# Weights quantised wholly beside the convolution, squares and layer norm sums on ScalarE, input turned by DMA

## The chip, the cores and the metric

One core of a Trainium2 chip runs the whole program in one launch. The metric is device time in microseconds, from the first instruction to the last. Engines are named as the profile names them: PE (matrix products), PEld (its weight loads), DVE (vector), ACT (scalar), POOL (GpSimd), SP (the engine that issues the DMAs here).

## The reference

```python
x = x + tanh(g_xattn[0]) * ssm(ctx, ctx, layernorm(x))          # x, ctx: [8, 512, 1024]
x = x + tanh(g_ffn[0]) * ffn(layernorm(x))
# ssm(k, v, q): 64 heads of 8 channels, sequence length 1024
kv  = einsum('bhil,bhjl->bijhl', k, v)                          # k = v = ctx here
out = causal_conv(kv, ssm_kernel[h]) + kv * D[h]
out = einsum('bijhl,bhil->bjhl', out, q)
# ffn: 1024 -> 4096 -> 1024; mx_quant: blocks of 32 along the contraction share a power of two
h = bf16(layernorm(x) * w + b)
h = gelu(bf16(mx_quant(h) @ mx_quant(W1) + b1))
h = bf16(mx_quant(h) @ mx_quant(W2) + b2)
ffn = bf16(x + h)
```

## The kernel before, in words

Two blocks run one after the other, with a barrier between them. Each engine has its own instruction list, in an order written out by hand; semaphores are the only link.

**The convolution block** (`mixer_block`) goes over 64 heads; two heads share a tile of x (32 tiles). For head h:
- ACT copies k into PSUM (`copy_k`). DVE multiplies it with shifted k into `kk`, 8 blocks of 4.5 diagonals of 64 columns (`make_kk`). ACT rounds `kk` to `kk_hi` (`high_half`), DVE makes the rest `kk_lo` (`low_half`). `kk` exists once, `kk_hi` and `kk_lo` twice.
- PE (`conv_stretch`) multiplies a Toeplitz slab of the taps, loaded by SP from `taps_scratch`, with `kk_hi` and `kk_lo` into a row of 2304 columns of PSUM (`y_ps`), in five stretches from the end of the row: 72 matmuls a head. After stretch 1 the upper part (blocks 5 to 7) is complete, at the end the lower part (blocks 0 to 4).
- DVE multiplies each part with q (`times_q`: part 0 is blocks 5 to 7, part 1 is blocks 0 to 4). POOL adds up the products in seven additions for each part (`sum_part`). PE turns the sums back, DVE adds x (`residual`, at odd heads), SP stores x1.
- At even heads DVE takes the layer norm statistics of the next x tile (`ln_stats`) and ACT applies them (`ln_apply`); at odd heads PE turns the result (`turn_q`) and ACT copies it out (`take_q`).

DVE's order in head h is: `times_q(h-1, 1)`, `make_kk(h+1)`, `ln_stats` (even) or `residual` (odd), `times_q(h, 0)`, `low_half(h+1)`, then a piece of weight work. That piece is, for heads 0 to 31, the block maxima of one weight tile (`weight_maxima`, 1 MB each), at head 32 also the scales of all weights (`weight_scales`), and from head 32 on the quantisation of one tile of W2 for each two heads: integers at the even head, clip and scale at the odd one (`layer2_ints`, `layer2_clip`, `layer2_quant`). In PSUM `y_ps` begins 256 columns into a bank.

**The FFN block** (`ffn_block`) goes over 16 groups of two x1 tiles (256 rows). For group g PE runs `layer1(g, b)` for 16 banks (256 matmuls) and then `layer2` of the two tiles of group g-1 (256 matmuls). ACT adds the bias and applies gelu; DVE takes statistics, weighs and quantises the input of group g+1 (`weigh_input`, `quantise_input`), takes the peaks of the hidden values (`peak`), quantises them (`hidden_ints`, `hidden_clip`, `hidden_quant`), and finishes the output tiles (`second_bias`, `gated_sum`). The quantised input `hq` is turned by PE (`turn_input`, 8 transposes for a tile, between the parts of `layer2`) and copied by ACT (`keep_input`) into `xq_T`, which exists once. In group 0 DVE also quantises the 16 tiles of W1, PE turns them (`turn_weights`) and ACT keeps them (`keep_w1`). SP loads x1 tiles (`load_tile`), stores an output tile (`store`, which waits for `gated_sum`) and loads the next tile into the same buffer (`reload`, which waits until that store has landed).

Of the kernel before, what the change touches and what calls it, by code (L numbers as in the profile page):

```python
# [16 lines left out]
P = 128  # L17
B = 8
# [17 lines left out]
W_BUFS = 4  # L36
# [3 lines left out]
L1_BANKS = 3  # L40
# [22 lines left out]
def mixer_block(nc, x_t, ctx_e, taps_in, skip_in, g_x, scratch, x1_t, w_m, w_raw, w_inv, w2_t, w2_raw, w2_int, w2_q,  # L63
                first_loads, tiles):

# [7 lines left out]
    half = tiles // 2  # L73
    stretches = [(max(end - 512, 0), end) for end in range(row, 0, -512)]
    with ExitStack() as stack:
# [6 lines left out]
        def sem(name):  # L82
# [3 lines left out]
        taps = sb("taps", [HEADS, PADK], F32)  # L86
        taps_hi = sb("taps_hi", [HEADS, PADK], F32R)
# [15 lines left out]
        stats = sb("stats", [P, 2, 6], F32)  # L103
        mean_var = sb("mean_var", [P, 2], F32)
# [30 lines left out]
        stats_ready, aggr_ready, var_ready, rstd_ready = sem("stats_ready"), sem("aggr_ready"), sem("var_ready"), sem("rstd_ready")  # L135
# [9 lines left out]
        def _(sp):  # L145
# [42 lines left out]
            sp.wait_ge(kk_ready, 1)  # L188
            load_k(2)
            for t in range(2, X_SLOTS):  # L190
                load_x(t)
            load_w(0)
            load_w(1)
            for h in range(heads):
# [11 lines left out]
                if 1 <= h < tiles - 1:  # L206
                    sp.wait_ge(w_max_ready, h)
                    load_w(h + 1)
                if h in (tiles - 2, tiles - 1):
                    load_w2(h - (tiles - 2))  # L210
                if t > half:
                    if h % TILE_HEADS == 0:
                        store_w2(t - half - 1)
                    elif t + 1 < tiles:
                        load_w2(t - half + 1)
# [11 lines left out]
        def _(pe):  # L227
            def conv_stretch(h, i):
# [7 lines left out]
                if i == 1 and h >= 1:  # L236
                    pe.wait_ge(products_ready, 2 * h)
# [43 lines left out]
        def _(act):  # L281
# [24 lines left out]

            def ln_apply(t):
# [3 lines left out]
                if t >= 1:  # L311
# [833 lines left out]
```

## Time and profile before

| | us |
|---|---|
| median of 3 runs (2044.01 to 2044.49) | 2044.43 |
| the profiled execution's own time | 2045.5 |
| its span | 2043.7 |
| PE busy | 1931.1 (94%) |
| DVE busy | 1735.5 (85%) |
| POOL busy | 967.6 (47%) |
| ACT busy | 735.7 (36%) |
| mean granted clock of PE | 0.977 |

Durations below come from the profiled execution. An engine's busy time says only how much it did; what sets the end is the wait that ends last in each stage. Idle time in square brackets stands before an instruction and names what ended it.

### The profile page before, as it was taken

What the parts mean: (1) busy time and instruction counts of PE and PEld (TensorE: products, weight loads), DVE (VectorE), ACT (ScalarE), POOL (GpSimd) and SP (SyncE); (2) the same over time, 40 slices, a digit from 0 to 9 for tenths busy, and PEclk for the clock granted to TensorE, in tenths of its full rate; (3) what the DMA queues carried; (4) which work ended last, traced back from release to release, by engine and by line L of the source; (5) the groups of instructions that cost most, each with busy time, mean ns of one, the idle gap of its engine ahead of it and who ended that gap; (6) DMA issues with size and microseconds to landing.
All of it is one profiled execution on the core that took longest, in us unless ns stands there. A gap on an engine that the chain in (4) does not pass through costs nothing. (4 is left out here: it accounts for less than half of the span.)

```text
span 2043.7 us, 29510 instructions
## 1 busy us (share of the span) xinstructions
PE 1931.1 (94%) x11776; PEld 1488.6 (73%) x11776; DVE 1735.5 (85%) x2092; ACT 735.7 (36%) x1028; POOL 967.6 (47%) x1036
## 2 busy tenths in 40 slices
PE   6999999999999999999826599999999999999998
PEld 5888888888788888888725466677776666667763
DVE  6888898898899999999779979888888888888843
ACT  3232222222222222222126444545544444455540
POOL 3888888888899999999912000000000000000000
PEclk9999999999999999999958799999999999999999
DMA  6555555555354555544437401111111111111111
GB/s 220 188 201 195 195 192 195 196 200 211 127 181 175 182 174 177 190 165 168 164 124 278 166 31 51 43 63 63 63 63 63 42 52 63 63 42 52 42 42 73
DMA packets 65769, 264.40 MB, mean 129 GB/s; under 512 B 7712, under 2 KB 7712, under 8 KB 57440
## 3 DMA queue, kind: packets, MB, share of 16 engines
q1 hardware_dynamic: 65632, 262.52, 36.1%
q8 instruction: 93, 1.52, 0.3%
q14 instruction: 44, 0.36, 0.1%
HBM read 219.96 MB, written 42.53 MB: 128 GB/s over the span
## 5 line engine op out<-in xcount | busy, mean ns | idle before, releaser
L242 PE MATMUL y_ps<-kk_hi,slab 128*128 128x512 f32 (+8 forms) x3072 | 872.9, 367 | 9.3 <-DMA slab<-taps_scratch 5.2
L242 PEld LDWEIGHTS y_ps<-kk_hi,slab 128*128 128x128 f32 x3072 | 559.2, 189 | 106.3 <-DMA slab<-taps_scratch 5.6
L242 PE MATMUL y_ps<-kk_lo,slab 128*128 128x512 f32 (+8 forms) x1536 | 563.0, 367 | 0.0
L714 PE MATMUL l_ps<-f_xq_T,w_T 128*128 128x256 bf16 x4096 | 461.4, 276 | 16.3 <-ACT arena L793 13.6
L714 PEld LDWEIGHTS l_ps<-f_xq_T,w_T 128*128 128x128 bf16 x4096 | 404.7, 99 | 70.3 <-ACT arena L793 13.9
L729 PE MATMUL acc_ps<-w_T,arena 128*128 128x512 bf16 x2048 | 449.0, 379 | 0.0
L729 PEld LDWEIGHTS acc_ps<-w_T,arena 128*128 128x128 bf16 x2048 | 199.2, 98 | 231.8
L1059 POOL TENSOR_TENSOR f_rstd<-f_var_eps,f_neg_half 128x1 f32<-128x1 f32 x32 | 23.4, 733 | 716.0 <-DVE f_var_eps L857 716.0
L242 PEld LDWEIGHTS y_ps<-kk_lo,slab 128*128 128x128 f32 x1536 | 290.5, 189 | 47.9
L793 ACT ACTIVATE arena<-l_ps,f_b 128x256 bf16<-128x256 f32 x512 | 214.3, 473 | 221.1 <-PE l_ps L714 215.3
L508 POOL TENSOR_TENSOR lsum<-lower 128x240 f32<-128x240 f32 (+1 forms) x128 | 252.5, 1973 | 73.4 <-DVE lower L384 73.4
L378 DVE TENSOR_TENSOR upper<-y_ps,q_ext 128x768 f32<-128x768 f32 (+1 forms) x128 | 155.9, 1218 | 98.2 <-PE y_ps L242 98.2
L289 ACT COPY k_ps<-k_ext 128x512 f32<-128x512 f32 x64 | 37.8, 591 | 508.1 <-DVE kk L359 498.8
L509 POOL TENSOR_TENSOR upper<-upper 128x384 f32<-128x384 f32 (+1 forms) x128 | 205.0, 1602 | 0.0
L364 DVE TENSOR_TENSOR kk_lo<-kk,kk_hi 128x2304 fp32r<-128x2304 f32 x64 | 163.5, 2555 | 2.8 <-ACT kk_hi L295 2.8
L356 DVE TENSOR_TENSOR kk<-k_ps,k_ext 128x2048 f32<-128x2048 f32 x64 | 145.7, 2276 | 0.0
L295 ACT CAST kk_hi<-kk 128x2304 fp32r<-128x2304 f32 x64 | 135.8, 2123 | 7.3 <-DVE kk L359 7.3
L511 POOL TENSOR_TENSOR lsum<-lsum,lower 128x240 f32<-128x240 f32 (+1 forms) x128 | 128.8, 1006 | 0.0
L800 ACT ACTIVATE arena<-arena 128x2048 bf16<-128x2048 bf16 x64 | 122.2, 1910 | 0.5
L384 DVE TENSOR_TENSOR lower<-y_ps,q_ext 128x576 f32<-128x576 f32 (+1 forms) x128 | 121.0, 945 | 0.0
L520 POOL TENSOR_TENSOR mixed<-upper 128x192 f32<-128x192 f32 (+1 forms) x128 | 94.4, 738 | 18.6 <-POOL upper L517 0.4
L513 POOL TENSOR_TENSOR upper<-upper 128x192 f32<-128x192 f32 (+1 forms) x128 | 95.9, 749 | 0.0
(109 smaller groups left out, 1901.1 us busy)
## 6 DMA issues: line engine op xcount, KB each, us to landing
slab<-taps_scratch SPq DMA_DIRECT2D x128, 512.0 KB, 4.4
arena<-in_w_m SPq DMA_DIRECT2D x32, 1024.0 KB, 6.6
arena<-x_scratch SPq DMA_DIRECT2D x64, 512.0 KB, 4.2
k_ext<-in_ctx_e SPq DMA_DIRECT2D x64, 384.0 KB, 3.0
arena<-in_w SPq DMA_DIRECT2D x24, 1024.0 KB, 6.5
x_tile<-in_x_t SPq DMA_DIRECT2D x32, 512.0 KB, 4.5
x_scratch<-x SPq DMA_DIRECT2D x32, 512.0 KB, 2.9
out_t<-arena SPq DMA_DIRECT2D x32, 512.0 KB, 2.6
```

The lines of the kernel that those rows point to most:

```text
L242: mm = nc.tensor.matmul(y_ps[:, y_base + begin:y_base + end], slab[s][:, half, d * P:(d + 1) * P], kk_part[s][:, begin - d * PAIR:end - d ...
L295: nc.scalar.copy(kk_hi[h % 2][:], kk[:].rearrange("p n c -> p (n c)")).then_inc(hi_ready, 1)
L356: nc.vector.tensor_tensor(view(kk, 0, [(PAIR, LB), (CH, DIAG), (1, CH)]), view(k_ps, 0, [(CH, LB), (0, DIAG), (1, CH)]), view(k, 0, [(EXT, ...
L364: nc.vector.tensor_tensor(kk_lo[h % 2][:], kk[:].rearrange("p n c -> p (n c)"), kk_hi[h % 2][:].bitcast(F32), ALU.subtract).then_inc(lo_re ...
L378: nc.vector.tensor_tensor(view(up, 0, [((DIAG + 1) * CH, count), (CH, DIAG), (1, CH)]), view(y_ps, y_at, [(PAIR, count), (CH, DIAG), (1, C ...
L508: add(lsum[:, :, B:], low[:, :, 0, B:], low[:, :, 1, B:], ALU.add).then_inc(lower_two, 1)
L509: add(up[:, :, 0:2, :], up[:, :, 0:2, :], up[:, :, 2:4, :], ALU.add).then_inc(upper_two, 1)
L511: add(lsum[:, :, B:], lsum[:, :, B:], low[:, :, 2, B:], ALU.add).then_inc(lower_all, 1)
L714: mm = nc.tensor.matmul(l1_ps[bank % L1_BANKS][:, a, :], w1_T[:, k, col:col + P], xq_T[:, k, :], start=(k == 0), stop=(k == L // P - 1))
L729: mm = nc.tensor.matmul(acc_ps[s][:, c * 512:(c + 1) * 512], hidden[g % 2][:, k, s * P:(s + 1) * P], w2_T[:, k, c * 512:(c + 1) * 512], st ...
L793: done = nc.scalar.activation(hidden[g % 2][:, c, :], l1_ps[bank % L1_BANKS][:, a, :], ACT.Identity, bias=b1_c[:, c:c + 1])
L800: nc.scalar.activation(h, h, ACT.Gelu_apprx_tanh).then_inc(gelu_ready, 1)
```

## The change

In the convolution block:
- `make_kk` leaves out the first diagonal (the squares), 512 of 2304 columns; ACT makes them (`squares`), and `high_half` and `low_half` wait for it.
- `ln_stats` moves from DVE to ACT: a pass with a running sum, the mean, a pass of squares with a running sum. It stands between `copy_k` and `squares` in ACT's list at even heads. POOL makes the variance.
- All 32 tiles have their maxima taken in heads 0 to 20 (three tiles in two heads), the scales follow at head 20, and all 32 tiles (W2, then W1) are quantised in heads 22 to 63, three tiles in four heads, and stored. For W1 the inverses are turned by PE in heads 22, 24, 26 and 28.
- `y_ps` begins 96 columns into a bank, so a stretch ends where part 0 begins: widths 352, 512, 512, 512 and 416, 78 matmuls a head. PE waits for part 1's products of the head before only ahead of stretch 2, not 1.

In the FFN block:
- W1 is loaded already quantised and turned; DVE's, PE's and ACT's work on it in group 0 is gone.
- `turn_input` leaves PE, `keep_input` leaves ACT: SP issues a DMA that turns `hq` into `xq_T`, two for each group, behind the group's `store` and `reload`.
- `layer1` has four banks in turn, not three.

```diff
-    stretches = [(max(end - 512, 0), end) for end in range(row, 0, -512)]
+    y_base = -PARTS[0][0] * PAIR % 512
+    edges = [0] + list(range(512 - y_base, row, 512)) + [row]
+    stretches = list(zip(edges[:-1], edges[1:]))[::-1]
...
-                if i == 1 and h >= 1:
+                if i == 2 and h >= 1:
                     pe.wait_ge(products_ready, 2 * h)
...
+            def squares(h):
+                act.wait_ge(k_loaded[h % 2], 16 * (h // 2) + 16)
+                if h >= 1:
+                    act.wait_ge(lo_ready, h)
+                    act.wait_ge(hi_ready, h)
+                nc.scalar.activation(kk[:, :, 0:CH], k_ext[h % 2][:, :, 0:CH], ACT.Square).then_inc(squares_ready, 1)
...
+            def ln_stats(t):
...
+                nc.scalar.activation(xn[:], x, ACT.Identity, accum_out=x_sum[:]).then_inc(sum_ready, 1)
+                act.wait_ge(sum_ready, t + 1)
+                nc.scalar.activation(neg_mean[:], x_sum[:], ACT.Identity, scale=-1.0 / L).then_inc(mean_ready, 1)
+                act.wait_ge(mean_ready, t + 1)
+                nc.scalar.activation(xn[:], x, ACT.Square, bias=neg_mean[:], accum_out=x_var[:]).then_inc(square_ready, 1)
...
                 if h + 2 < heads:
                     copy_k(h + 2)
+                if h % TILE_HEADS == 0 and t + 1 < tiles:
+                    ln_stats(t + 1)
                 if h + 1 < heads:
+                    squares(h + 1)
                     high_half(h + 1)
...
+                for n in maxima_of[h]:
+                    weight_maxima(n)
+                if h == scales_head:
                     weight_scales()
...
+                for n in range(2 * W_TILES):
+                    if n in ints_of[h]:
+                        weight_ints(n)
+                    if n in quant_of[h]:
+                        weight_quant(n)
...
+            def turn_input(t):
+                s, g = t % GROUP, t // GROUP
+                sp.wait_ge(x_quant, t + 1)
+                if g >= 1:
+                    sp.wait_ge(l1_ready, banks * g)
+                sp.dma_start(xq_T[:, :, s * P:(s + 1) * P], hq[s][:], transpose=True).then_inc(input_turned[s], 16)
...
                 if 1 <= g <= groups:
                     store(GROUP * (g - 1))
                     reload(GROUP * (g - 1) + 1)
+                for s in range(GROUP):
+                    if g + 1 < groups:
+                        turn_input(GROUP * (g + 1) + s)
```

ACT in the convolution block, an even head (first four rows) and an odd one, before:

```order
L289 COPY k_ps<-k_ext 128x512 [waits kk_ready,k_loaded0]
L295 CAST kk_hi<-kk 128x2304 [waits y_ready,kk_ready]
L309 ACTIVATE shift<-neg_mean,rstd 128x1 [waits rstd_ready]
L313 ACTIVATE xn<-x_tile,shift,rstd 128x1024 [waits q_turned,shift_ready]
L289 COPY k_ps<-k_ext 128x512 [waits kk_ready,k_loaded1]
L295 CAST kk_hi<-kk 128x2304 [waits y_ready,kk_ready]
L303 COPY q_ext<-turn_ps 128x8x64 [waits products_ready,q_turned]
```

The same place now (the even head is the first eight rows):

```order
L328 COPY k_ps<-k_ext 128x512 [waits kk_ready,k_loaded0]
L359 ACTIVATE xn,x_sum<-x_tile 128x1024 [waits q_turned,x_loaded2]
L361 ACTIVATE neg_mean<-x_sum 128x1 [waits sum_ready]
L363 ACTIVATE xn,x_var<-x_tile,neg_mean 128x1024 [waits mean_ready]
L335 ACTIVATE kk<-k_ext 128x8x64 [waits hi_ready,lo_ready,k_loaded1]
L342 CAST kk_hi<-kk 128x2304 [waits y_ready,kk_ready,squares_ready]
L367 ACTIVATE shift<-neg_mean,rstd 128x1 [waits rstd_ready]
L369 ACTIVATE xn<-x_tile,shift,rstd 128x1024 [waits shift_ready]
L328 COPY k_ps<-k_ext 128x512 [waits kk_ready,k_loaded1]
L335 ACTIVATE kk<-k_ext 128x8x64 [waits hi_ready,lo_ready,k_loaded0]
L342 CAST kk_hi<-kk 128x2304 [waits y_ready,kk_ready,squares_ready]
```

Between the copy of k and the rounding of `kk`, an even head now has four more instructions on ACT and an odd one has one more.

SP in the FFN block, one steady group, before:

```order
L634 DMA arena<-x_scratch 128x1024 [waits f_n_ready]
L643 DMA out_t<-arena 128x1024 [waits f_out_ready]
L639 DMA arena<-x_scratch 128x1024 [waits f_out_stored]
L634 DMA arena<-x_scratch 128x1024 [waits f_n_ready]
L643 DMA out_t<-arena 128x1024 [waits f_out_ready]
L639 DMA arena<-x_scratch 128x1024 [waits f_out_stored]
```

And now:

```order
L698 DMA arena<-x_scratch 128x1024 [waits f_n_ready]
L707 DMA out_t<-arena 128x1024 [waits f_out_ready]
L703 DMA arena<-x_scratch 128x1024 [waits f_out_stored]
L698 DMA arena<-x_scratch 128x1024 [waits f_n_ready]
L707 DMA out_t<-arena 128x1024 [waits f_out_ready]
L703 DMA arena<-x_scratch 128x1024 [waits f_out_stored]
L714 DMA_TRANSPOSE f_xq_T<-f_hq 128x8x128 [waits f_l1_ready,f_x_quant] x2
```

The two DMAs that turn the next group's input stand last, behind the group's second store (tile 2(g-1)) and the reload that waits for that store to land.

## Rows read from the trace of the kernel before

**Rows 1.** Stretches: us; busy PE, PEld, DVE, ACT, POOL; PE clock; DMA share; GB/s.

```profile
19.20:1016.10 996.90, 992.68 (x5104) 848.04 (x5104) 894.46 (x872) 264.47 (x311) 902.74 (x916) 1.00 0.53 183
1016.10:1219.90 203.80, 119.05 (x952) 88.94 (x953) 180.41 (x249) 88.16 (x121) 32.11 (x39) 0.79 0.42 155
...
539.20:546.00 6.80, 5.88 (x14) 4.62 (x15) 5.35 (x5) 2.64 (x2) 5.71 (x7) 0.50 0.28 96
```

**Rows 2.** Timeline of DVE over two heads: start us, us, instruction, [idle before].

```profile
765.47 2.59 DVE L364 TENSOR_TENSOR kk_lo<-kk,kk_hi 128x2304 fp32r<-128x2304 f32 x1
...
771.08 1.48 DVE L378 TENSOR_TENSOR upper<-y_ps,q_ext 128x1280 f32<-128x1280 f32 x1
...
773.94 2.27 DVE L356 TENSOR_TENSOR kk<-k_ps,k_ext 128x2048 f32<-128x2048 f32 x1
...
779.13 0.96 DVE L378 TENSOR_TENSOR upper<-y_ps,q_ext 128x768 f32<-128x768 f32 x1 [0.91 <-PE y_ps L242]
...
780.94 2.55 DVE L364 TENSOR_TENSOR kk_lo<-kk,kk_hi 128x2304 fp32r<-128x2304 f32 x1
783.40 2.79 DVE L413 TENSOR_TENSOR arena<-arena,b_b 128x2048 int16<-128x2048 f32 x1
...
791.51 1.12 DVE L448 TENSOR_TENSOR x<-turn_ps,x_tile 128x512 f32<-128x512 f32 x1
...
796.39 2.59 DVE L364 TENSOR_TENSOR kk_lo<-kk,kk_hi 128x2304 fp32r<-128x2304 f32 x1
```

**Rows 3.** Timeline of ACT in the same two heads.

```profile
776.63 0.59 ACT L289 COPY k_ps<-k_ext 128x512 f32<-128x512 f32 x1 [7.41 <-DVE kk L359]
777.16 2.12 ACT L295 CAST kk_hi<-kk 128x2304 fp32r<-128x2304 f32 x1
781.34 0.30 ACT L309 ACTIVATE shift<-neg_mean,rstd 128x1 f32<-128x1 f32 x1 [2.06 <-POOL rstd L495]
781.67 1.25 ACT L313 ACTIVATE xn<-x_tile,shift,rstd 128x1024 f32<-128x1024 f32 x1
```

**Rows 4.** Timeline of POOL in the same two heads.

```profile
784.00 3.06 POOL L509 TENSOR_TENSOR upper<-upper 128x384 f32<-128x384 f32 x1
```

**Rows 5.** Groups of DVE instructions by shape, heads 2 to 32: count, busy, mean ns.

```profile
L404 DVE TENSOR_REDUCE w_max<-arena 128x64 f32<-128x2048 f32 x31 | 70.6, 2277 | 0.0
```

**Rows 6.** Timeline of PE at head 33, behind the weight scales.

```profile
540.12 0.79 PE L242 MATMUL y_ps<-kk_hi,slab 128*128 128x512 f32 x1 [4.14 <-DVE lower L384]
```

**Rows 7.** Timeline of PE over one steady FFN group.

```profile
1502.25 0.93 PE L714 MATMUL l_ps<-f_xq_T,w_T 128*128 128x256 bf16 x7
...
1544.45 0.61 PE L690 MATMUL tr_ps<-f_ident,f_hq 128*128 128x128 bf16 x8
...
1558.71 0.49 PE L714 MATMUL l_ps<-f_xq_T,w_T 128*128 128x256 bf16 x3
```

**Rows 8.** Timeline of DVE in the same group: last peaks, gated sum.

```profile
1533.29 0.69 DVE L916 TENSOR_SCALAR f_weighted<-arena 128x2048 uint16<-128x2048 uint16 x1
...
1553.24 1.28 DVE L971 SCALAR_TENSOR_TENSOR arena<-f_o_res,f_gate_tanh,arena 128x1024 f32<-128x1024 bf16 x1
```

**Rows 9.** Timeline of SP in the same group: the second store and its reload.

```profile
1554.55 0.34 SPq L643 DMA_DIRECT2D out_t<-arena  x1
1557.18 0.32 SPq L639 DMA_DIRECT2D arena<-x_scratch  x1
```

**Rows 10.** DMA issues of the page: count, KB each, median us to landing.

```profile
arena<-in_w_m SPq DMA_DIRECT2D x32, 1024.0 KB, 6.6
...
out_t<-arena SPq DMA_DIRECT2D x32, 512.0 KB, 2.6
```

**Rows 11.** Timeline of PE: last turn of the convolution, layer 1 of group 2.

```profile
1025.71 1.11 PE L264 MATMUL turn_ps<-ident,mixed 128*128 128x128 f32 x4 [9.66 <-POOL mixed L520]
...
1219.91 2.35 PE L714 MATMUL l_ps<-f_xq_T,w_T 128*128 128x256 bf16 x20
```

**Rows 12.** Timeline of DVE behind the second quantised input tile.

```profile
1057.20 1.22 DVE L991 TENSOR_TENSOR arena<-arena,b_b 128x2048 bf16<-128x2048 int16 x1
```

More of the change, by code:

```diff
@@ L72, in mixer_block @@
     row = LB * PAIR
-    half = tiles // 2
-    stretches = [(max(end - 512, 0), end) for end in range(row, 0, -512)]
+    maxima_heads = 2 * (2 * W_TILES) // 3
+    scales_head = maxima_heads - 1
+    quant_head = maxima_heads
+    spread_heads = [quant_head + quant_head % 2 + 2 * i for i in range(4)]
+    maxima_of = [[] for h in range(heads)]
+    for n in range(2 * W_TILES):
+        maxima_of[n // 3 * 2 + (n % 3 == 2)].append(n)
+    ints_of, quant_of = [[] for h in range(heads)], [[] for h in range(heads)]
+    for n in range(2 * W_TILES):
+        ints_of[quant_head + (4 * n + 1) // 3].append(n)
+        quant_of[min(quant_head + (4 * n + 3) // 3, heads - 1)].append(n)
+    y_base = -PARTS[0][0] * PAIR % 512
+    edges = [0] + list(range(512 - y_base, row, 512)) + [row]
+    stretches = list(zip(edges[:-1], edges[1:]))[::-1]
     with ExitStack() as stack:
@@ L191, in _ @@
                 load_x(t)
-            load_w(0)
-            load_w(1)
+            for n in range(W_SLOTS):
+                load_w(n)
             for h in range(heads):
@@ L205, in _ @@
                         load_x(t + 3)
[L206 to L215, printed above, removed]
+                if h >= 2:
+                    for n in quant_of[h - 2]:
+                        if n + W_SLOTS < 2 * W_TILES:
+                            load_w(2 * W_TILES + n + W_SLOTS)
+                if h >= 1:
+                    for n in maxima_of[h - 1]:
+                        load_w(n + W_SLOTS)
+                    for n in quant_of[h - 1]:
+                        store_w(n)
             for parity in range(2):
@@ L218, in _ @@
             first_loads(sp)
-            store_w2(tiles - half - 1)
+            for n in quant_of[heads - 1]:
+                store_w(n)
             store_x1(tiles - 1)
-            sp.wait_ge(w2_stored, 16 * (tiles - half))
+            for stored in w_stored:
+                sp.wait_ge(stored, 16 * (2 * W_TILES // W_SLOTS))
             for parity in range(2):
@@ L749, in _ @@
                             layer2(GROUP * (g - 1) + s, part)
-                        if s == 0 and g + 1 < groups:
-                            turn_input(GROUP * (g + 1) + part)
         @block.scalar
         def _(act):
-            def keep_w1(j):
-                for b in range(2):
-                    act.wait_ge(turned, 2 * j + b + 1)
-                    col = (2 * j + b) * P
-                    nc.scalar.copy(w1_T[:, :, col:col + P], w_turned_ps[2 * (j % 2) + b]).then_inc(kept, 1)
-            def keep_input(t):
-                s, g = t % GROUP, t // GROUP
-                act.wait_ge(input_turned, t + 1)
-                if g >= 1:
-                    act.wait_ge(l1_ready, banks * g)
-                nc.scalar.copy(xq_T[:, :, s * P:(s + 1) * P], tr_ps[:]).then_inc(input_kept, 1)
             def first_norm(t):
@@ L832, in _ @@
                     norm_again(GROUP * (g - 1))
-                for s in range(GROUP):
-                    if g + 1 < groups:
-                        keep_input(GROUP * (g + 1) + s)
                 for s in range(GROUP):
```

366 lines of the change are left out of this document (162 added, 204 removed).

## Prediction

> **What bounds the kernel now.** I read the stretches first, then the timelines of one pair of heads and one FFN group, engine by engine.
>
> In the convolution PE is busy for 992.7 of 996.9 us at full granted clock, DVE for 894 and POOL for 903 [rows 1]. So PE is the bound and the other two are close behind. Two heads take 30.92 us: the distance between two `low_half` of the same parity, 765.47 and 796.39 [rows 2]. In each head DVE still waits some 0.9 us for PE ahead of the first product [rows 2]: that is all its slack. ACT is three quarters idle, but its place in the chain counts: DVE's `kk` is ready at 776.63, ACT copies k, rounds, and is done at 779.28 (777.16 + 2.12) [rows 3], before DVE has finished `times_q(h, 0)` and asks for it at 780.94 [rows 2]. This wait is hidden by 1.7 us.
>
> In the FFN one group takes 56.46 us (1502.25 to 1558.71), PE without a gap [rows 7]. Between the two, from 1016.1 to 1219.9, PE is busy for only 119 of 204 us at a mean clock of 0.79 [rows 1]: DVE quantises W1 there. That is what the change can win.
>
> **Convolution, pair by pair.** Starts of neighbouring rows give DVE's steps: part 1's products 2.86 us (771.08 to 773.94), part 0's 1.81 (779.13 to 780.94), `low_half` 2.46 (780.94 to 783.40), integers 2.79 less an overlap of 0.08, so 2.71; clip and scale 3.15 (765.47 to 771.08 is 5.61, less the low half) [rows 2]. `kk` is ready 5.55 us after part 1's products began (771.08 to 776.63) [rows 2, 3]. Without the squares its large multiplication has 1536 of 2048 values: 2.27 becomes 1.70, and the 5.55 becomes 4.98. Residual: about 2.1. Maxima: 2.28 a tile less overlap, 2.2 [rows 5].
>
> Now the even head. Behind `kk` ACT has: copy 0.53; a pass over 1024 values 1.25; the mean 0.30; a second pass 1.25; the squares, 512 values as the copy, 0.59; rounding 2.12; four handovers at some 0.05. Together 6.2 us [rows 3], where it was 2.7. (No row shows an ACT pass with a running sum; at least 1.25, and I allow up to 0.3 more each for the range.) DVE's products of part 0 hide 1.8 of it. So `kk_hi` comes 4.98 + 6.2 = 11.2 us after the head's start on DVE, `kk_lo` at 13.7. The odd head isn't touched: 4.9 + 2.1 + 1.8 + 2.5 = 11.2. A pair is 24.9 us plus weight work, and what waits behind `low_half` on DVE is everything of the next head.
> - Heads 0 to 19, three maxima: 24.9 + 6.6 = 31.5 against 30.92. Ten pairs, +6, less 2 for what PE has in hand at the start: **+4**.
> - Heads 20 and 21, the scales: they stall PE by 4.14 us [rows 6] before and, I take it, now: **0**.
> - Heads 22 to 61, three tiles for two pairs of heads twice over, so 1.5 tiles a pair: 1.5 × (2.71 + 3.15) = 8.8, in all 33.7 against 30.92. Twenty pairs: **+55**, PE idle for nearly 3 us in each.
> - Head 63 ends with two quantisations and one set of integers (9 us) between its two products; the last ones come some 5 us later, of which I count 3 as not yet in the pairs: with rounding **+1 to 3**.
>
> PE itself does the same number of columns; 78 matmuls for 72, fewer of them 512 wide. I count nothing; PE's own need stays near 30.8 a pair and is hidden under 33.7. The later wait for part 1's products (stretch 2) is what makes the uneven heads possible, but buys no time where DVE is the bound. Sum of this block: **+60**.
>
> POOL decides whether it is more. An addition of 384 values that lies beside DVE's integers takes 3.06 us [rows 4]; the same engine is 903 of 997 us busy already [rows 1]. With 1.5 tiles a pair for 1 (second half) more of its work stands still. The Trainium skill (SBUF — State Buffer, Who interferes with whom) says that a DVE instruction with two SBUF inputs contends with a GpSimd instruction that reads SBUF, one with a single input does not; by this rule the low halves and the weight products would hold POOL up and the squares taken from DVE would give it nothing back. From rows: 903 us over 32 pairs is 28.2 in the mean, with half a tile; an addition held up costs some 2 us, and integers and scale hold up one each, so 3 to 4 a tile: 26.4 without, 31 to 33 with 1.5 tiles, just under DVE's 33.7. I leave it at that, with up to +1.5 a pair in the range.
>
> **Start of the FFN.** From the last turn (1025.71) to layer 1 of group 2 (1219.91) it is 194.2 us [rows 11]. Now: the second input tile was quantised at 1057.20 [rows 12], 31.5 behind the turn; without the first weight tile's integers and clip ahead of it 2.7 less: 28.8. One DMA turn, 4: group 0 starts at +33. Its 28 us of matmuls (28.1 a group, half of the 56.46) plus 3 for a clock still at 0.5: +64. Two turns, 6: group 1 at +70. From the end of layer 1 of group 0 DVE has: waiting for the gelu (2); last peak to gated sum as in a steady group, 21.2 (1533.29 to 1554.52 [rows 8]), less the output tile's 3 that group 0 lacks; two more statistics (3.5); its list for group 1 up to the gated sum, an estimated 43 of the 52.3 below, since it has no idle time in front; then store, reload and turns (9): group 2 at +140, say 139. Against 194: **-55**.
>
> **A steady group.** Follow it from the start of layer 1 (1502.25). DVE's gated sum ends at 1554.52 (1553.24 + 1.28) [rows 8]; from the last peak at 1533.29 it has no pause. SP stores at 1554.55, and can reload only when the store has landed, 1557.18, plus 0.32 to issue [rows 9]. Only then come the two turns. So they start 55.3 us behind the start of layer 1, and the next layer 1 needs both. PE would be done at 55.6 (56.46 less two turns of 0.45 each [rows 7]). In the old order the turns lay in the middle of layer 2; now the whole transfer is bare.
>
> No row shows a DMA that turns. Lower bound: two issues (0.34) and one landing like the store from SBUF, 2.6 us [rows 9, 10]: 2.9. Upper: two 1 MB loads one after the other, 6.6 each [rows 10]: 13.2. I take the store's row, since it too reads SBUF, twice in series with its issue: **6.0**. (The reload's 512 KB lie ahead of them in the same queue.) The Trainium skill (Advanced Engine Details and Errata, X-Bar Transpose (TRN2)) says that TRN2's transposing DMAs are as fast as plain ones, at 350 to 400 GB/s. By it two tiles of 256 KB would take 1.5 us of transfer, and the turns would be near my lower bound (an estimate). No run here shows a turn by DMA yet.
>
> PE then stands still for 5.7 us in each group. What follows is shown behind head 33: after an idle time of 4.14 us that began at 535.98 [rows 6] the granted clock was 0.5, the 1.2 GHz level, from 539.20 to 546.00 [rows 1]: from 3.2 to 10 us behind the start of the idle time. Layer 1 would run in it for 4.3 us and lose 2.1, and since DVE's list hangs on layer 1's banks, the loss goes on. A group: 55.3 + 6.0 + 2.1 = 63.4, +6.9. Thirteen of them between groups 2 and 15: **+90**; the last group's clock: **+2**.
>
> **Sum.** 2043.7 + 60 - 55 + 90 + 2 = 2140.7 for the span. The execution's span is 0.7 below the median of the runs, so **2141**.
>
> **Rivals.**
> 1. Forecast: ACT's longer list and the bare turns both cost. Chance 0.48; its own range 2085 to 2215 (turns 3.5 to 11 us, pairs 33 to 35).
> 2. Convolution as forecast, but turns at the lower bound, 2.9: +1.7 to +3.4 a group (the clock may still fall) and 3 less at the start: 2141 - 90 - 3 + 22 to 44 = 2070 to 2092. For it: a plain 512 KB store needs only 2.6. Chance 0.10.
> 3. Slow turns: their issue or transfer takes 13 us or more together. Then +13 or more a group, 2141 + 13 × 7 = 2232 and up. Nothing in the rows excludes it. Chance 0.14.
> 4. Convolution keeps PE's pace (ACT's passes overlap more than I think), turns as forecast: about 2081. Chance 0.08.
> 5. The other side, by one mechanism: the turns don't stand behind the gated sum, because DVE reaches it earlier than 52.3 us behind layer 1 once ACT's copies and PE's turns are gone. Then a group is PE's 55.6, -0.9 × 13 = -12, and the sum is 2044 + 60 - 58 - 12 = 2034. It decides from a group of 56 us down. If pairs of heads also stay near 31, some 1975. For it: DVE has idle time early in the group, ahead of the second bias, which waits for ACT. Against it: that wait hangs on layer 1's bank 2, so it moves with layer 1. Chance 0.18, mixed cases included.
> 6. All effects cancel to within 0.2% (which is about what a measurement can tell): 0.02.
>
> Faster 0.18, same 0.02, slower 0.80. Rivals 5 and 3 lie outside at the ends: a range from 2030 to 2235 leaves out about 0.2.
>
> **What would show it.** In the heads behind 22 `kk_lo` should wait for ACT's `kk_hi` by 4 us at even heads, and a pair should be 33.7; PE should be idle once a pair, ahead of an odd head, waiting for `kk_lo`. ACT's rows should read 1.25 for each of the two passes. In the FFN the first matmul of each layer 1 should wait for the DMA on `xq_T` for some 6 us, with a clock of 0.5 behind it, and SP should issue the turns directly behind the reload. Layer 1 of group 2 should start about 140 us behind the last turn. Wrong would be: a pair at 31, POOL as releaser of most waits, turns issued ahead of the store, or a landing far from 3 us.

## The result, and the profile after

The changed kernel took 2121.81 us (median of 4 runs, 2119.38 to 2123.69) where the kernel before took 2044.46 in the same session: 1.0378 times as long, 95% interval 1.0365 to 1.0391. Its profiled execution took 2121.0 us, with a span of 2118.9 against 2043.7.

The page of the changed kernel (busy time and its share of the span; then the groups of instructions: count, busy, mean ns, idle time ahead and what ended most of it):

```profile
PE 1932.1 (91%) x11632; PEld 1517.0 (72%) x11680; DVE 1671.2 (79%) x1947; ACT 799.4 (38%) x1196; POOL 1009.0 (48%) x1069
...
L268 PE MATMUL y_ps<-kk_hi,slab 128*128 128x352 f32 (+6 forms) x3328 | 905.1, 353 | 32.3 <-issue 27.3
...
L771 PE MATMUL l_ps<-f_xq_T,w_T 128*128 128x256 bf16 x4096 | 483.3, 284 | 113.8 <-DMA f_xq_T<-f_hq 106.9
...
L443 DVE TENSOR_TENSOR kk_lo<-kk,kk_hi 128x2304 fp32r<-128x2304 f32 x64 | 168.3, 2630 | 82.8 <-ACT kk_hi L342 82.7
```

PE is as busy as before (1932.1 against 1931.1 us), so all of the 75 us is idle time. Two groups hold most of PE's idle time: 106.9 us in which layer 1 waits for the DMA that turns its input, 15 times, and 32.3 us inside the convolution, of which 27.3 stand as "issue" (the engine waited for nothing that the profile shows). DVE waits for ACT's `kk_hi` for 82.7 us; only part of that can reach PE.

**Where the convolution lost.** `low_half` writes `kk_lo` once a head, so its starts mark the heads. On DVE, heads 20, 24, 44 and 62, first of the kernel before, then of the changed one:

```profile
325.65 2.55 DVE L364 TENSOR_TENSOR kk_lo<-kk,kk_hi 128x2304 fp32r<-128x2304 f32 x1
...
387.48 2.55 DVE L364 TENSOR_TENSOR kk_lo<-kk,kk_hi 128x2304 fp32r<-128x2304 f32 x1
...
703.65 2.58 DVE L364 TENSOR_TENSOR kk_lo<-kk,kk_hi 128x2304 fp32r<-128x2304 f32 x1
...
981.87 2.58 DVE L364 TENSOR_TENSOR kk_lo<-kk,kk_hi 128x2304 fp32r<-128x2304 f32 x1
```

```profile
327.56 2.56 DVE L443 TENSOR_TENSOR kk_lo<-kk,kk_hi 128x2304 fp32r<-128x2304 f32 x1
...
394.52 2.84 DVE L443 TENSOR_TENSOR kk_lo<-kk,kk_hi 128x2304 fp32r<-128x2304 f32 x1
...
719.77 2.55 DVE L443 TENSOR_TENSOR kk_lo<-kk,kk_hi 128x2304 fp32r<-128x2304 f32 x1
...
1025.94 2.57 DVE L443 TENSOR_TENSOR kk_lo<-kk,kk_hi 128x2304 fp32r<-128x2304 f32 x1
```

The lag is 1.9 us at head 20, 7.0 at 24, 16.1 at 44, 44.1 at 62. The last turn of the convolution comes at 1071.46 against 1025.71 [rows 11]: 45.8 late. So the ten pairs with W2 (24 to 44) take 32.5 us each and the nine with W1 (44 to 62) 34.0, against 30.92 [rows 2].

ACT in one even head of the part with W1, where [rows 3] had a copy and a rounding:

```profile
764.57 0.59 ACT L328 COPY k_ps<-k_ext 128x512 f32<-128x512 f32 x1 [9.10 <-DVE kk L437]
765.09 1.06 ACT L359 ACTIVATE xn<-x_tile 128x1024 f32<-128x1024 f32 x1
766.06 0.18 ACT L359 ACTIVATION_READ_ACCUMULATOR xn<-x_tile 128x1 f32 x1
...
766.51 1.15 ACT L363 ACTIVATE xn<-x_tile,neg_mean 128x1024 f32<-128x1024 f32 x1
...
768.31 2.12 ACT L342 CAST kk_hi<-kk 128x2304 fp32r<-128x2304 f32 x1
```

DVE's `kk_lo` behind it, and then PE's first matmul of the next head:

```profile
770.53 2.56 DVE L443 TENSOR_TENSOR kk_lo<-kk,kk_hi 128x2304 fp32r<-128x2304 f32 x1 [3.43 <-ACT kk_hi L342]
```

```profile
773.19 0.40 PE L268 MATMUL y_ps<-kk_hi,slab 128*128 128x352 f32 x1 [1.77 <-issue]
```

From the copy of k (764.57) to the end of the rounding (770.43) ACT needs 5.86 us, where it was 2.65. DVE stands 3.43 us; `kk_lo` ends at 773.09 and PE, idle for 1.77 us, goes on at 773.19. A running sum adds an instruction of its own, 0.18 us, behind each pass.

With W2 another engine was full as well (us; busy PE, PEld, DVE, ACT, POOL; PE clock; DMA share; GB/s):

```profile
378.00:700.00 322.00, 310.49 (x1738) 277.41 (x1737) 276.80 (x245) 126.36 (x175) 314.62 (x297) 1.00 0.56 193
```

POOL is busy for 314.6 of 322 us and waits for nothing there. With W1, from 740 to 1025 us, it is busy for 266.0 of 285 and waits 12.6 us for DVE's products.

**Where the FFN won and lost.** PE from the convolution's last turn to the second steady group, then SP at the end of that group, then the turning DMAs in the list of transfers (count, median us to landing):

```profile
1071.46 1.97 PE L301 MATMUL turn_ps<-ident,mixed 128*128 128x128 f32 x8 [11.54 <-POOL mixed L600]
1103.36 30.09 PE L771 MATMUL l_ps<-f_xq_T,w_T 128*128 128x256 bf16 x256 [29.93 <-DMA f_xq_T<-f_hq]
1145.85 10.05 PE L771 MATMUL l_ps<-f_xq_T,w_T 128*128 128x256 bf16 x64 [12.41 <-DMA f_xq_T<-f_hq]
...
1211.04 30.84 PE L771 MATMUL l_ps<-f_xq_T,w_T 128*128 128x256 bf16 x256 [4.96 <-DMA f_xq_T<-f_hq]
...
1274.55 0.69 PE L771 MATMUL l_ps<-f_xq_T,w_T 128*128 128x256 bf16 x3 [5.04 <-DMA f_xq_T<-f_hq]
```

```profile
1266.11 0.34 SPq L707 DMA_DIRECT2D out_t<-arena  x1
1268.74 0.32 SPq L703 DMA_DIRECT2D arena<-x_scratch  x1
1269.16 3.25 SPq L714 DMA_TRANSPOSE f_xq_T<-f_hq  x2
```

```profile
f_xq_T<-f_hq SPq DMA_TRANSPOSE x32, 4.5
```

From the last turn to layer 1 of group 2 it is 139.6 us against 194.2 [rows 11]. Layer 1 of group 3 then stands idle for 5.04 us: the store goes at 1266.11, the reload, which waits for it to land, at 1268.74, the turns from 1269.16 on, and layer 1 starts 5.4 us later. Thirteen groups, from 1211.04 to layer 1 of group 15 at 2029.22, take 818.2 us, 62.9 each, against 56.46 [rows 7].

### The profile page after: what moved, and what is told of

Same layout as the page of the kernel before. It is cut to its first block and busy times, and to the rows that moved or that the text cites. A ratio compares the mean times of both kernels' runs of the same rounds, so it can differ in the third digit from the quotient of the medians.

```text
span 2118.9 us, 29533 instructions
## 1 busy us (share of the span) xinstructions
PE 1932.1 (91%) x11632; PEld 1517.0 (72%) x11680; DVE 1671.2 (79%) x1947; ACT 799.4 (38%) x1196; POOL 1009.0 (48%) x1069
## 5 line engine op out<-in xcount | busy, mean ns | idle before, releaser
L268 PE MATMUL y_ps<-kk_hi,slab 128*128 128x352 f32 (+6 forms) x3328 | 905.1, 353 | 32.3 <-issue 27.3
L268 PEld LDWEIGHTS y_ps<-kk_hi,slab 128*128 128x128 f32 x3328 | 602.1, 190 | 104.2 <-issue 30.3
L771 PE MATMUL l_ps<-f_xq_T,w_T 128*128 128x256 bf16 x4096 | 483.3, 284 | 113.8 <-DMA f_xq_T<-f_hq 106.9
L268 PE MATMUL y_ps<-kk_lo,slab 128*128 128x512 f32 (+6 forms) x1664 | 583.6, 351 | 0.0
L268 PEld LDWEIGHTS y_ps<-kk_lo,slab 128*128 128x128 f32 x1664 | 316.6, 190 | 34.4
L443 DVE TENSOR_TENSOR kk_lo<-kk,kk_hi 128x2304 fp32r<-128x2304 f32 x64 | 168.3, 2630 | 82.8 <-ACT kk_hi L342 82.7
L589 POOL TENSOR_TENSOR upper<-upper 128x384 f32<-128x384 f32 (+1 forms) x128 | 222.7, 1740 | 0.0
L588 POOL TENSOR_TENSOR lsum<-lower 128x240 f32<-128x240 f32 (+1 forms) x128 | 158.2, 1236 | 60.4 <-DVE lower L463 60.4
L984 DVE TENSOR_TENSOR f_o_res<-f_o_res 128x1024 bf16<-128x1024 bf16 x32 | 22.1, 692 | 186.6 <-ACT f_o_res L817 186.0
L600 POOL TENSOR_TENSOR mixed<-upper 128x192 f32<-128x192 f32 (+1 forms) x128 | 151.8, 1186 | 18.6 <-POOL upper L597 0.4
L809 ACT ACTIVATE f_n<-arena,f_shift,f_rstd 128x1024 bf16<-128x1024 f32 x32 | 39.7, 1240 | 295.3 <-POOL f_shift L1045 295.3
```

The costliest lines, as they stand in the source:

```text
L268: mm = nc.tensor.matmul(y_ps[:, y_base + begin:y_base + end], slab[s][:, half, d * P:(d + 1) * P], kk_part[s][:, begin - d * PAIR:end - d ...
L443: nc.vector.tensor_tensor(kk_lo[h % 2][:], kk[:].rearrange("p n c -> p (n c)"), kk_hi[h % 2][:].bitcast(F32), ALU.subtract).then_inc(lo_re ...
L588: add(lsum[:, :, B:], low[:, :, 0, B:], low[:, :, 1, B:], ALU.add).then_inc(lower_two, 1)
L589: add(up[:, :, 0:2, :], up[:, :, 0:2, :], up[:, :, 2:4, :], ALU.add).then_inc(upper_two, 1)
L600: add(out, rows[0], rows[4], ALU.add).then_inc(sums_ready, 1)
L771: mm = nc.tensor.matmul(l1_ps[bank % L1_BANKS][:, a, :], w1_T[:, b, k, a * P:(a + 1) * P], xq_T[:, k, :], start=(k == 0), stop=(k == L // ...
```

## Experiments

**1. The turns first in SP's list.** One move in SP's loop:

```diff
                 if g + 2 < groups:
                     load_tile(GROUP * (g + 2) + 1)
+                for s in range(GROUP):
+                    if g + 1 < groups:
+                        turn_input(GROUP * (g + 1) + s)
                 if 1 <= g <= groups:
                     store(GROUP * (g - 1))
                     reload(GROUP * (g - 1) + 1)
-                for s in range(GROUP):
-                    if g + 1 < groups:
-                        turn_input(GROUP * (g + 1) + s)
```

> The changed kernel, with SP issuing the two DMAs that turn the next group's input ahead of the group's even store and its reload, not behind them. Theory (the turns are bare because they stand behind the gated sum, the store and the reload): a group falls from 63 us to PE's own 55.6, PE's idle time ahead of layer 1 goes, the granted clock stays at full; 13 groups save about 95 us: 2027 us. Rival (DVE's list from layer 1 to the gated sum is itself the bound, and the turns only end last beside it): a group stays at 58 us or more, 2055 or more. Second rival (the turns are slow by themselves, by their queue): PE goes on waiting for them, about 2100.

Measured: 2020.49 us (2020.01 to 2020.96), 0.9886 of before, interval 0.9866 to 0.9906; 101 us less than the changed kernel. PE in a steady group, then SP:

```profile
1206.72 28.11 PE L771 MATMUL l_ps<-f_xq_T,w_T 128*128 128x256 bf16 x256
...
1262.29 1.91 PE L771 MATMUL l_ps<-f_xq_T,w_T 128*128 128x256 bf16 x16
```

```profile
1234.90 2.61 SPq L714 DMA_TRANSPOSE f_xq_T<-f_hq  x2
1259.05 0.34 SPq L707 DMA_DIRECT2D out_t<-arena  x1
```

The turns go out at 1234.90, 0.1 us behind the end of layer 1, and lie under 27.5 us of layer 2; the next layer 1 follows without a gap. The group is 55.57 us for 62.94, so thirteen groups give 95.8 us. The order in SP's list was worth 101 us in all, and with it the change as a whole is 1.1% faster than the kernel before.

**2. The statistics ahead of the copy of k.** ACT does its passes while DVE still makes `kk`:

```diff
-                if h + 2 < heads:
-                    copy_k(h + 2)
                 if h % TILE_HEADS == 0 and t + 1 < tiles:
                     ln_stats(t + 1)
+                if h + 2 < heads:
+                    copy_k(h + 2)
```

> The changed kernel, with ACT's layer norm statistics at even heads ahead of the copy of k, in time in which ACT waits anyway, not behind it. Theory (the four instructions between the copy and the rounding make kk_lo late): DVE no longer waits for kk_hi, a pair of heads falls from 31.3 (maxima), 32.4 (W2) and 34 (W1) to PE's 30.8 or close to it, the last turn of the convolution comes 40 to 50 us earlier: about 2077 us. Rival (POOL, held up by DVE's quantisation, bounds the pairs from head 22 on): pairs stay at 32 and more, at most 15 us are won: 2107 or more.

Measured: 2109.33 us (2109.24 to 2109.43), ratio 1.0321 (1.0300 to 1.0342): 12.5 less than the changed kernel. `kk_lo` at heads 20, 44 and 62:

```profile
323.34 2.56 DVE L443 TENSOR_TENSOR kk_lo<-kk,kk_hi 128x2304 fp32r<-128x2304 f32 x1
...
717.21 2.56 DVE L443 TENSOR_TENSOR kk_lo<-kk,kk_hi 128x2304 fp32r<-128x2304 f32 x1
...
1012.88 2.62 DVE L443 TENSOR_TENSOR kk_lo<-kk,kk_hi 128x2304 fp32r<-128x2304 f32 x1
```

Four us are won up to head 20, and 2.8 of them are lost again up to head 24. The pairs with W2 stay (from 394.52 to 719.77 before the edit, from 393.05 to 717.21 with it), though DVE's wait for ACT falls from 26.7 us to 5.8 between 378 and 700 us: so with W2 ACT's chain did not set the pace in the changed kernel. Those with W1 go from 34.0 to 32.9. The wait for ACT was real, but beside it stands another bound at some 32.4 to 32.9 us a pair. The theory that ACT's chain was most of the loss fell; its rival, POOL, was what the next runs had to test.

**3. Both edits.**

> Both edits together: statistics ahead of the copy of k, turns ahead of the store. Theory: the gains add, since they lie in different blocks: 2122 - 95 - 45 = 1982 us, 3% faster than the kernel before. Under the POOL rival for the convolution about 2012, under the DVE rival for the groups about 2010, under both 2045.

Measured: 2008.13 us (2007.19 to 2009.39), ratio 0.9827 (0.9811 to 0.9844), faster than either kernel. PE's last turn and layer 1 of group 2 (134.1 us apart), then three stretches: with the maxima, with W2, with W1 (us; busy PE, PEld, DVE, ACT, POOL; PE clock; DMA share; GB/s):

```profile
1059.18 1.97 PE L301 MATMUL turn_ps<-ident,mixed 128*128 128x128 f32 x8 [9.80 <-POOL mixed L600]
...
1193.28 1.91 PE L771 MATMUL l_ps<-f_xq_T,w_T 128*128 128x256 bf16 x16
```

```profile
60.00:350.00 290.00, 290.00 (x1620) 260.29 (x1619) 254.82 (x218) 111.59 (x155) 247.64 (x280) 1.00 0.62 227
378.00:700.00 322.00, 310.88 (x1727) 276.75 (x1726) 282.46 (x243) 128.44 (x177) 313.74 (x298) 0.99 0.57 193
740.00:1000.00 260.00, 248.58 (x1363) 220.20 (x1361) 234.08 (x206) 97.33 (x136) 254.01 (x239) 1.00 0.55 189
```

With the maxima PE has no gap and a pair is 30.8 us. With the quantisation POOL is busy for 313.7 of 322 and 254.0 of 260 us, and PE misses 11 us in each. How DVE holds POOL up: the same 3 us on both, POOL first.

```profile
814.46 3.19 POOL L593 TENSOR_TENSOR upper<-upper 128x320 f32<-128x320 f32 x1
817.61 2.92 POOL L595 TENSOR_TENSOR upper<-upper,lsum 128x320 f32<-128x320 f32 x1
```

```profile
814.29 2.62 DVE L443 TENSOR_TENSOR kk_lo<-kk,kk_hi 128x2304 fp32r<-128x2304 f32 x1
816.84 2.96 DVE L487 TENSOR_TENSOR arena<-arena,w_max 128x2048 int16<-128x2048 f32 x1
```

An addition of 320 values that takes 0.89 us with nothing beside it takes 3.19 while DVE makes `kk_lo` (both inputs in SBUF), and the next one 2.92 beside the integers.

**4. Both edits, but the row where it was before** (256 columns into a bank, 72 matmuls a head, wait at stretch 1):

```diff
-    y_base = -PARTS[0][0] * PAIR % 512
-    edges = [0] + list(range(512 - y_base, row, 512)) + [row]
-    stretches = list(zip(edges[:-1], edges[1:]))[::-1]
+    y_base = -row % 512
+    stretches = [(max(end - 512, 0), end) for end in range(row, 0, -512)]
...
-                if i == 2 and h >= 1:
+                if i == 1 and h >= 1:
```

> Both edits, and the row in PSUM again 256 columns into a bank, with stretches of 512, 512, 512, 512 and 256 columns and PE waiting for part 1's products of the head before ahead of stretch 1. Theory (the later wait carries the uneven weight work of odd heads: 5.9 us of it on DVE against 2.9): PE has 5.4 us from a head's start to that wait where it has 8.3 now, and waits 1.5 to 3 us in each odd-to-even step from head 22 on: 21 pairs, 30 to 60 us slower than both, about 2025. Rival (DVE is never that late once the statistics don't hold it up): within 5 us of both.

Measured: 2018.78 us (2017.07 to 2020.49), 10.7 slower than with the moved row; ratio 0.9878 (0.9858 to 0.9898). That lies between the two expectations. The stretch with the maxima:

```profile
60.00:350.00 290.00, 285.75 (x1469) 242.70 (x1468) 249.12 (x211) 112.84 (x156) 249.03 (x277) 1.00 0.61 225
```

The 10 us are lost in the maxima heads (31.7 us a pair against 30.8), where the theory had put them behind head 22. The waits for part 1's products that it foresaw there exist (9.4 us between 378 and 700 us) but cost nothing: a pair with quantisation is 32.4 and 32.5, for 32.4 and 32.8 with the new row. That fits POOL setting it (experiment 5). Only 4.3 of the 9 us lost in this stretch are idle time in PE's rows; where the rest goes stays open.

**5. POOL with one addition fewer.** Of the seven additions the one of rows 0 and 1 is left out, so one term of the sums is missing:

```diff
-                pool.wait_ge(upper_two, n + 1)
-                add(rows[0], rows[0], rows[1], ALU.add).then_inc(upper_all, 1)
...
-                pool.wait_ge(upper_all, n + 1)
+                pool.wait_ge(upper_two, n + 1)
```

> Both edits (turns first in SP's list, statistics ahead of the copy of k) with one addition fewer on POOL in each part of each head: rows 0 and 1 of the upper products are not added, so one term in five of the sums is left out. DVE's, ACT's and PE's lists are those of the kernel with both edits (2008.1 us; pairs of heads 30.9 us with maxima, 32.0 to 33.1 with quantisation). Theory: POOL's additions, held up by DVE's instructions with two inputs in SBUF, bound the pairs with quantisation; freed of some 1.5 us a head, POOL falls under PE, and the pairs go to 31.0 to 31.4: 21 pairs by 1.2 to 1.7, so 1972 to 1983 us, and DVE has no waits for POOL. Rival: DVE's own list or ACT's rounding bounds them, POOL only keeps pace: pairs stay at 32 or over, 2003 to 2008 us.

Measured: 1971.18 us (1970.35 to 1971.68), 37 less than with both edits; ratio 0.9639 (0.9623 to 0.9656). The two stretches with quantisation:

```profile
378.00:700.00 322.00, 321.97 (x1812) 288.58 (x1812) 296.65 (x258) 132.14 (x181) 304.58 (x272) 1.00 0.60 202
740.00:1000.00 260.00, 259.00 (x1436) 231.47 (x1435) 245.70 (x217) 97.81 (x133) 243.69 (x216) 1.00 0.55 185
```

And PE's last turn of the convolution, 36.4 us ahead of the one in experiment 3 and 2.9 ahead of [rows 11]:

```profile
1022.82 1.97 PE L301 MATMUL turn_ps<-ident,mixed 128*128 128x128 f32 x8 [9.55 <-POOL mixed L598]
```

PE has hardly a gap any more, though DVE and ACT have the same lists as in experiment 3. Pairs go from 32.4 and 32.8 to 31.1 and 31.2. DVE's busy time for a pair stays (share of the stretch times the pair: 28.4 before this edit and 28.6 with it for W2, 29.5 and 29.5 for W1), so the gain is not DVE being held up less by POOL. So POOL bounded those pairs, not DVE and not ACT.

**6. The W1 scales made once**, for the first tile only (the other 15 use them):

```diff
-                    nc.vector.tensor_scalar(w1_scale.bitcast(U16), inv_T[:, j * 2 * P:(j + 1) * 2 * P].bitcast(U16),
+                    if j == 0:
+                        nc.vector.tensor_scalar(w1_scale.bitcast(U16), inv_T[:, j * 2 * P:(j + 1) * 2 * P].bitcast(U16),
...
-                    dve.wait_ge(w1_scaled, n - W_TILES + 1)
+                    dve.wait_ge(w1_scaled, 1)
```

> Both edits, and the scales of a W1 tile (one instruction on DVE of 0.6 to 0.9 us for each tile) are made for the first tile only, so the other 15 tiles of W1 are scaled by its scales. Theory (POOL bounds the pairs with quantisation): DVE's 0.7 us a tile is slack, 15 tiles bring 0 to 4 us: 2004 to 2008 us. Rival (DVE's list bounds the pairs with W1): 15 times 0.7 to 0.9 are won, 10 to 14 us: 1994 to 1998 us.

Measured: 2006.92 us (2006.61 to 2007.08), 1.2 less, no more than the runs of experiment 3 scatter; a pair with W1 goes from 32.8 to 32.7. DVE's work here was slack.

**7. The squares on DVE again**, `kk` in one instruction with its first diagonal, `squares` gone from ACT:

```diff
-                nc.vector.tensor_tensor(view(kk, CH, [(PAIR, LB), (CH, DIAG - 1), (1, CH)]),
-                                        view(k_ps, 0, [(CH, LB), (0, DIAG - 1), (1, CH)]),
-                                        view(k, B, [(EXT, LB), (B, DIAG - 1), (1, CH)]), ALU.mult)
+                nc.vector.tensor_tensor(view(kk, 0, [(PAIR, LB), (CH, DIAG), (1, CH)]),
+                                        view(k_ps, 0, [(CH, LB), (0, DIAG), (1, CH)]),
+                                        view(k, 0, [(EXT, LB), (B, DIAG), (1, CH)]), ALU.mult)
```

> Both edits, and the squares (first diagonal) are made by DVE again, with the other diagonals in one instruction; ACT has no squares. DVE's multiplication has 2048 values, not 1536: 0.57 us a head more on DVE, ACT's list between the copy of k and the rounding 0.6 us shorter. Theory (POOL, held up by DVE's instructions with two inputs in SBUF, bounds the pairs with quantisation): the multiplication reads PSUM and one SBUF tile and takes DVE's slack, so 0 to 15 us slower than 2008.1. Rival: ACT's chain bounds some heads, and it is a few us faster.

Measured: 2006.92 us (2006.64 to 2007.94), 1.2 less, which the scatter of the runs does not tell from nothing. Moving the squares to ACT, one of the change's parts, brings nothing in this list: the multiplication reads one operand from PSUM, and what it took of DVE was slack.

**8. The variance on ACT.** POOL's small instruction ahead of the power moves to ACT:

```diff
+                act.wait_ge(square_ready, t + 1)
+                act.wait_ge(half_ready, 2)
+                nc.scalar.activation(var_eps[:], x_var[:], ACT.Identity, bias=eps[:], scale=1.0 / L).then_inc(var_ready, 1)
...
-                pool.wait_ge(square_ready, t + 1)
-                nc.gpsimd.tensor_scalar(var_eps[:], x_var[:], 1.0 / L, EPS, ALU.mult, ALU.add).then_inc(var_ready, 1)
```

> Both edits, and ACT makes the variance plus epsilon (128x1) behind its pass of squares, where POOL made it; POOL has one instruction less for each tile of x, one that took 1.38 us in the mean (20 of them from 378 to 1050 us) since DVE's instructions hold it up. Theory (POOL bounds the pairs with quantisation; one addition of seven taken away brought 37 us, PE's pace being reached): 1.4 us less on POOL and 0.5 us more on ACT in each pair, so 20 pairs by 0.7 to 1.4: 14 to 28 us faster than 2008.1, 1980 to 1994 us. Rival: POOL's instruction is stretched only by an instruction of DVE that would stretch the next one of POOL in its place, so the 1.38 is really 0.3 us: 0 to 6 us faster.

Measured: 2002.00 us (2000.12 to 2002.38), 6.1 less than with both edits; ratio 0.9788 (0.9771 to 0.9804), the fastest kernel here that computes all of the reference. POOL from 740 to 1000 us, with both edits (the addition of row 4, the variance, the power) and then with this one more (that addition and the power):

```profile
L595 POOL TENSOR_TENSOR upper<-upper,lsum 128x320 f32<-128x320 f32 x16 | 42.4, 2648 | 0.0
...
L573 POOL TENSOR_SCALAR var_eps<-x_var 128x1 f32<-128x1 f32 x8 | 12.7, 1582 | 0.7
...
L575 POOL TENSOR_TENSOR rstd<-var_eps,neg_half 128x1 f32<-128x1 f32 x8 | 4.4, 550 | 0.7
```

```profile
L598 POOL TENSOR_TENSOR upper<-upper,lsum 128x320 f32<-128x320 f32 x16 | 51.0, 3186 | 0.0
...
L578 POOL TENSOR_TENSOR rstd<-var_eps,neg_half 128x1 f32<-128x1 f32 x8 | 16.5, 2062 | 0.0
```

The variance took 1.58 us in the mean, but with it gone the power takes 2.06 in place of 0.55 and the addition 3.19 in place of 2.65: the hold falls on whoever stands beside DVE's instruction. The rival's mechanism was right: what is won is about the instruction's own length with its handover, 6.1 us over the 20 tiles that have quantisation beside them, 0.3 each. Pairs go from 32.4 to 32.2 with W2 and from 32.8 to 32.4 with W1.

**9. Three banks in layer 1**, `L1_BANKS = 3` in place of 4, with both edits.

> Both edits, with three PSUM banks in turn in layer 1, as in the kernel before, not four: the one part of the change that no other run separates. Groups of the FFN are PE's own 55.57 us with four. Theory: three banks held a group to PE's pace in the kernel before (56.46 us with 16 transposes of 0.45 us, less those 55.6), so the group stays at 55.6 and the time within 3 us of 2008.1. Rival: with DVE's peaks and ACT's gelu closer together the fourth bank hides a wait in each group; then 0.3 us or more a group, 5 us or more in all.

Measured: 2010.17 us (2010.01 to 2010.63), 2.0 slower; ratio 0.9831 (0.9816 to 0.9845), not told apart from experiment 3 by the intervals. A steady group is 55.6 us with either, as the theory had it. The difference lies ahead of group 2: layer 1 of group 1, which waits 3.2 us for ACT in place of 1.5, takes 35.8 us from start to end for 32.4, and group 2 comes 137.5 us behind the last turn for 134.1. (The 0.45 us of the expectation is for a turn, eight transposes, not for one of them.)

## Why the prediction held, and where its terms were off

Forecast 2141, measured 2121.8, so the case that was called likeliest came about: ACT's longer list and the bare turns both cost. For the turns the mechanism was right too. In the convolution it was right in part: with W2 it was POOL, which the prediction had put just under the bound, that set the pairs. That its sum still came near there is partly luck, since the two bounds lie within 1.2 us a pair of each other (34.0 and 32.8 with W1). By its terms, of the span:

| term | forecast | measured |
|---|---|---|
| convolution | +60 | +45.8 |
| start of the FFN | -55 | -54.6 |
| thirteen groups | +90 | +84.1 |
| behind them | +2 | 0 |
| sum | +97 | +75.2 |

- **ACT's chain**: 6.2 us from the copy of k to the end of the rounding, measured 5.86; the passes take 1.06 and 1.15, not 1.25, and their running sums 0.18 each, which was allowed for. The wait ahead of `kk_lo` at even heads is there, 3.43 us at 770.53 and 2.7 in the mean with W2, for the 4 foreseen. (The odd head's terms add up to 11.3, not 11.2; 0.1 us a pair.)
- **Maxima heads**: 31.5 a pair, measured 31.3 once they are steady (15.67 and 15.65 us between heads) and 31.2 in the mean of the first ten; and the first ten pairs of before were not 30.92 either: they took 31.1. So it is only +1.9 at head 20, not +4.
- **The scales**: counted as 0. Heads 20 to 24 lose 5.1 us, while before had its own stall at heads 32 and 33, 7.0 us of its 316.2 from head 24 to 44 (ten pairs at 30.92 are 309.2). Together -1.8.
- **Heads 22 to 61**, the term that was mis-sized: 33.7 for all twenty pairs. With W1 it is 34.0: the scales of a W1 tile (0.81 us in the mean) were not counted, while clip and scale take 2.9 and not 3.15. With W2 it is 32.5: a tile costs DVE less there, clip and scale 0.77 and 1.54 us in the mean for the 3.15 of [rows 2], integers 2.44 for 2.79. With these the prediction's own sum would be some 32 us a pair (an estimate: 24.9 and 1.5 times 4.7), which lies under POOL's 32.4. That is 12 us over ten pairs.
- **POOL**: put at 31 to 33 a pair, "just under" DVE's 33.7 (its terms give 30.9 to 32.4). This step stood on an estimate of 26.4 us and 3 to 4 us a tile, and both hold: by the rows of experiment 3 POOL is busy for 26.3 us of a pair with maxima (247.6 of 290 us, times 30.75), 31.6 of one with W2 and 32.0 of one with W1. Its pace is 32.4 to 32.8. With W2 it was the bound in the changed kernel already, where the pair stays at 32.4 when ACT's wait goes; with W1 it became the bound as soon as that wait was gone (experiments 2, 3 and 5). The prediction named DVE and ACT as the bound throughout; of the 45.8 us lost in the convolution removing ACT's wait brings back only 10.8 (last turn at 1060.71 in experiment 2); with POOL relieved too all of it is back.
- The Trainium skill (SBUF — State Buffer, Who interferes with whom) lets a DVE instruction with two SBUF inputs contend with a GpSimd one that reads SBUF. The runs agree: 0.89 us becomes 3.19 beside `kk_lo`, and taking the squares off DVE (one input in PSUM) gave POOL nothing back (experiment 7). But the prediction's "one with a single input does not" is too wide for these runs. DVE's clip, with one SBUF input of int16, takes 0.69 us at 415.75 in the changed kernel and 1.35 at 790.35, where an addition of POOL that had been stretched to 2.99 us still had 0.8 to run; the scales of a W1 tile, also with one input, take 0.21 us at the least in experiment 3 and up to 1.03 in the changed kernel.
- **Start of the FFN**: -55, measured -54.6. Group 0 came at +31.9 (33), group 1 at +74.4, 4 later than the 70 said, where its turns stood behind 26 weight loads in SP's list: issued from 1133.54 on, they held SP for 10.3 us, and layer 1 started at 1145.85. Group 2 absorbed it.
- **A steady group**: 63.4, measured 62.9. The turns were put at 6.0 us and took 5.4: two issues of 1.6 in series, then a landing, not two landings in series. The clock did fall, and layer 1 takes 30.5 to 31.0 us and 29.6 to 29.8 in turn where it takes 28.11 in experiment 1: 2.2 lost in the mean of the thirteen groups, for 2.1. PE's own 55.6 us was right too (55.57 in experiment 1), though the 0.45 us a turn that gives it stands in no row; [rows 7] has 0.61.
- The Trainium skill (Advanced Engine Details and Errata, X-Bar Transpose (TRN2)) has transposing DMAs as fast as plain ones. By the transfer alone two turns would take 1.5 us (an estimate); the trace has 4.5 us to landing for one, where a plain store of twice the bytes lands in 2.6 [rows 10].
- **Rival 2**: its lower bound stood on the store's row and fell for that reason. (Two issues of 0.34 and a landing of 2.6 are 3.3, not 2.9.)
- **Rival 5**, the faster side, decided from a group of 56 us down. Experiment 1 reaches 55.57, but only by moving the turns: at 1259.05, 52.3 us behind layer 1, DVE's gated sum is just as late as [rows 8] had it. What the rival left out is that the turns need not stand behind it.
- **The moved row**: counted as nothing. In experiment 4 the old row costs 10.7 us, in the heads with maxima, once ACT's wait is gone. Whether it bought anything in the changed kernel itself no run shows.
- **The end**: no turn and no loss of clock behind the last group, 89.7 us as before.

## What to carry to other kernels

Moving a transpose from PE to a DMA cost nothing in the steady groups here only once the DMA was issued as soon as its input was ready: look what stands ahead of it in the issuing engine's list, and above all for a store that waits for the last work of the group. Read POOL's share not against the engine that waits but as a bound of its own: at 97%, with the additions that lie beside DVE's two-input instructions stretched up to threefold and more, it set the pace, though hardly a wait named it until the louder wait was removed. And taking one held-up instruction off such an engine brought only about that instruction's own length, since the hold moved to the next; a whole addition per part took it below the bound.

## What the runs showed of the hardware that was not expected

Granted clock (column PEclk) in two stretches of the changed kernel, one in the convolution and one at the start of layer 1 of group 3:

```profile
738.90:742.20 3.30, 3.30 (x12) 3.30 (x13) 3.30 (x2) 0.00 (x0) 3.30 (x2) 0.50 0.97 395
1274.75:1278.10 3.35, 3.35 (x18) 2.37 (x17) 0.00 (x0) 0.06 (x1) 0.00 (x0) 0.50 0.25 102
```

- In the convolution PE has idle times of 1 to 2.3 us about once a pair, and five times, between 738.9 and 981.2 us, a stretch of 3.4 us was granted 0.50, the 1.2 GHz level, with PE busy all through it. Each of the five began within 0.3 us of the end of an idle time of 1.7 to 2.3 us; other idle times of 1.7 us, as at 771.4, were not followed by one. In the FFN, with 5 us of idle time ahead of each layer 1, it was one such stretch of 3.4 us and one of 6.8 in turn, each beginning within 2 us of layer 1's start. Layer 1 (256 matmuls) then takes 29.6 to 31.0 us in place of 28.11.
- A turning DMA of 128x1024 bf16 from SBUF to SBUF holds SP for 1.6 us (two in 3.25 us), where the store's plain issue holds it for 0.34. Behind 26 weight loads two of them held it for 10.3 us.
- Contention works both ways: the same integers took 2.28 us on DVE beside a 128x1 instruction of POOL, and 2.79 beside an addition of 384 values. DVE in experiment 5, and POOL:

```profile
841.38 2.28 DVE L487 TENSOR_TENSOR arena<-arena,w_max 128x2048 int16<-128x2048 f32 x1
...
857.58 2.79 DVE L487 TENSOR_TENSOR arena<-arena,w_max 128x2048 int16<-128x2048 f32 x1
```

```profile
841.59 2.84 POOL L575 TENSOR_TENSOR rstd<-var_eps,neg_half 128x1 f32<-128x1 f32 x1
...
858.18 3.06 POOL L589 TENSOR_TENSOR upper<-upper 128x384 f32<-128x384 f32 x1
```
